# A banded attention and expert kernel on one core: TensorE's score steps in pairs

## The reference

```python
S = jnp.einsum('bcqd,bckd->bcqk', Qc, Kwin)              # local keys, 64 queries against 128
As = [S[:, :, qg, kg].reshape(bh, n, m)]                 # the band
for l in range(1, L + 1):                                # pooled keys, 8 a level
    Al = jnp.einsum('bcwd,bcpd->bcwp', q.reshape(bh, nbl, w, d), Kprev)
    As.append(Al.reshape(bh, n, p))
mn = maxes.min(axis=-1, keepdims=True)                   # the least of the five levels' maxima
exps = [jnp.exp(A - mn) for A in As]
...
out = jnp.einsum('bcqk,bckd->bcqd', Cfull, Vwin)         # value products, local
out = out + jnp.einsum('bcwp,bcpd->bcwd', Cs[l]..., Vprev)   # and pooled
...
x = x + _L0_attn_ref(_layernorm(x)); x = x + _L0_ffn_ref(_layernorm(x))
```

## Time and profile before

| | |
|---|---|
| median of 3 runs | 288.24 us (285.51 to 290.07) |
| the profiled execution's own time | 288.01 us |
| its span, first to last instruction | 286.2 us |
| outside the span | 1.8 us |
| TensorE busy | 273.4 us, 96% |
| mean granted TensorE clock | 0.964 of full speed |
| VectorE, ScalarE, GpSimd busy | 54%, 54%, 47% |
| attention units on TensorE | about 23 to 174 us |
| experts on TensorE | about 174 to 284 us |

### The profile page before, as it was taken

How to read it: one execution, slowest core, us unless ns; L and a number is a source line. 1 busy time by engine, 2 the same in 40 slices (tenths; PEclk the granted TensorE clock), 3 DMA queues, 4 the chain that set the end, 5 groups by cost and what they waited for, 6 DMA issues and landing times.

```text
span 286.2 us, 7298 instructions
## 1 busy us (share of the span) xinstructions
PE 273.4 (96%) x2705; PEld 226.5 (79%) x2705; DVE 154.6 (54%) x453; ACT 154.7 (54%) x316; POOL 135.8 (47%) x235
## 2 busy tenths in 40 slices
PE   7999999999999999993999999999999999999994
PEld 6868767887788988883888888788888678888883
DVE  7782644633344001322643162789886987777773
ACT  6765745534653432742487456544676555555551
POOL 7753302300041154140171301888885678888881
PEclk9999999989999975998999799999999999999999
DMA  7221176340097687558445011300000000000000
GB/s 212 61 58 60 57 171 192 81 126 2 11 289 277 168 229 170 145 155 165 128 144 154 26 22 21 85 10 10 10 11 9 10 11 10 9 11 18 11 9 19
DMA packets 19683, 24.14 MB, mean 84 GB/s; under 512 B 8312, under 2 KB 14456, under 8 KB 19648
## 3 DMA queue, kind: packets, MB, share of 16 engines
q1 hardware_dynamic: 18528, 22.80, 28.8%
q10 hardware_dynamic: 1120, 0.89, 1.2%
HBM read 11.91 MB, written 5.37 MB: 60 GB/s over the span
## 4 chain that ended last, share of the span: by engine, by line
PE 88%; DVE 3%; issue 3%; DMA 2%; SPq 1%; ACT 1%; POOL 1%; DVEq 0%; ACTq 0%; POOLq 0%
PE bank L1327 13%; PE bank L1140 12%; PE bank L1142 11%; PE bank L1141 11%; PE bank L1303 8%; PE bank L1306 6%; PE bank L1289 5%; PE bank L1221 3%; PE bank L1150 3%; PE bank L1331 2%; PE bank L1271 2%; PE bank L1237 2%; PE bank L1183 1%; DMA qst<-nshiftT 1%; PE bank L1171 1%
## 5 line engine op out<-in xcount | busy, mean ns | idle before, releaser
L752 POOL TENSOR_TENSOR work<-work 128x256 f32<-128x256 f32 x110 | 81.4, 744 | 31.2 <-DVE work L1123 18.3
L1123 DVE SCALAR_TENSOR_TENSOR work<-bank,comb,work 128x256 f32<-128x256 f32 x128 | 58.9, 480 | 24.7 <-ACT work L893 23.4
L893 ACT ACTIVATE work<-bank 128x256 f32<-128x256 f32 x128 | 48.4, 384 | 42.8 <-PE bank L1142 40.3
L868 ACT ACTIVATE work<-bank 128x512 f32<-128x512 f32 x64 | 37.7, 594 | 44.0 <-PE bank L1306 39.8
L1327 PE MATMUL bank<-work,vaug 128*64 128x64 f32 x1024 | 45.7, 235 | 0.0
L1327 PEld LDWEIGHTS bank<-work,vaug 128*64 128x64 f32 x1024 | 37.0, 144 | 9.0 <-issue 1.6
L658 POOL COPY vaug<-vwin 128x64 f32<-128x64 f32 x64 | 13.2, 250 | 51.7 <-PE bank L1331 51.5
L1303 PE MATMUL bank<-bar,ident_r 128*128 128x512 f32 x64 | 34.1, 533 | 0.0
L1306 PEld LDWEIGHTS bank<-qmk,kst 98*128 98x128 f32 x128 | 26.4, 206 | 4.3 <-issue 1.0
L1306 PE MATMUL bank<-qmk,kst 98*128 98x256 f32 x128 | 27.3, 297 | 0.0
L1141 PE MATMUL bank<-arena,xT_hi 128*128 128x512 f32 x64 | 25.1, 392 | 0.0
(11 more groups left out here) (217 smaller groups left out, 532.4 us busy)
## 6 DMA issues: line engine op xcount, KB each, us to landing
w_stage<-w SPq DMA_DIRECT2D x8, 512.0 KB, 3.9
qmk<-qst SPq DMA_DIRECT2D x20, 96.0 KB
qst<-arena SPq DMA_DIRECT2D x12, 128.0 KB, 3.8
kst<-arena SPq DMA_DIRECT2D x9, 128.0 KB, 3.2
qst<-q_rows SPq DMA_DIRECT2D x3, 384.0 KB, 4.2
qmk<-q_rows SPq DMA_DIRECT2D x12, 96.0 KB
p_rows<-kpool SPq DMA_DIRECT2D x2, 512.0 KB, 4.5
attT<-denom SPq DMA_DIRECT2D x8, 128.0 KB, 2.8
```

The lines of the kernel that those rows point to most:

```text
L752: gp.tensor_tensor(gacc[t % 2][:, :], gacc[t % 2][:, :], gtmp[(adds - 1) % TMP_RING][:, :], ALU.add).then_inc(acc_done, 1)
L868: act.activation(prob[lo % P_RING][:, :, :, :], bank[sc % SCORE_BANKS][:, :].rearrange("p (c j q) -> p c j q", c=2, j=GH), ACT.Exp).then_i ...
L893: act.activation(sig[hn % SIG_RING][:, :], bank[hn % HID_BANKS][:, HID:2 * HID], ACT.Sigmoid).then_inc(sig_done, 1)
L1123: dve.scalar_tensor_tensor(dst[:, :], bank[hn % HID_BANKS][:, 0:HID], comb[:, t, e:e + 1], sig[hn % SIG_RING][:, :], ALU.mult, ALU.mult).t ...
```

## The change

The loop over the ten score steps of a unit goes in pairs. Both score steps of a pair are put into the list first, then as many out steps as are due (two in the steady state), and then all side work that was hung beside the first and the second of them. The order among the score steps, among the out steps and among the side steps stays. SP's own order stays.

```diff
     for u in range(UNITS):
-        for i in range(SPU):
-            s.append(("score", u, i))
-            if unmasked:
-                mask()
-            if i >= 2:
-                local.append((u, i - 2))
-                unmasked.append((u, i - 2))
-            if len(local) > LAG:
+        for i in range(0, SPU, 2):
+            for n in (i, i + 1):
+                s.append(("score", u, n))
+                if unmasked:
+                    mask()
+                if i >= 2:
+                    local.append((u, n - 2))
+                    unmasked.append((u, n - 2))
+            while len(local) > LAG:
                 attend()
-            s += beside.get(u, {}).get(i, [])
-            if u + 1 < UNITS:
-                first = GUARD_AT[u]
-                if first <= i < first + 2:
-                    s.append(("guard", u + 1, i - first))
-                if i == first + 1:
-                    s.append(("shift", u + 1))
-                if i == first + 2:
-                    s.append(("shiftT", u + 1))
-                if i == first + 3:
-                    s.append(("shift load", u + 1))
+            for n in (i, i + 1):
+                s += beside.get(u, {}).get(n, [])
+                if u + 1 < UNITS:
+                    first = GUARD_AT[u]
+                    if first <= n < first + 2:
+                        s.append(("guard", u + 1, n - first))
+                    if n == first + 1:
+                        s.append(("shift", u + 1))
+                    if n == first + 2:
+                        s.append(("shiftT", u + 1))
+                    if n == first + 3:
+                        s.append(("shift load", u + 1))
```

## The result

| | before | changed |
|---|---|---|
| median beside each other | 287.78 us (285.51 to 290.07, 4 runs) | 294.50 us (292.98 to 297.00, 4 runs) |
| ratio, 95% interval | | 1.0269 (1.0160 to 1.0378) |
| profiled execution, its span | 288.01 us, 286.2 us | 294.15 us, 292.4 us |
| mean granted TensorE clock | 0.964 | 0.942 |

The account below looks back on a forecast made before the run. TensorE, busy 273.4 of 286.2 us, was taken as the bound. From 288.0 us, pairing wins 10.2, of which 7.8 are lost to later sources and growing waits, leaving −2.4: 285.6 us, range 281.5 to 290.0.

Parts of the forecast that it names:

- a rival with 0.22: New waits in units 1 and 2 bring more falls of TensorE's clock: 287.3 to 290 us, chance 0.22.
- other slices at half: Sign that the forecast is wrong: TensorE's clock at half in other slices than the four of the trace before.
- The price of a fall: One fall of TensorE's clock costs 1.8 us, from the 23rd slice of the trace before (1.4 to 2.1).
- The second row that lay ready: Stretch from 104 to 113 us before, at granted clock 0.50, where work takes up to twice as long.
- the section on short idle spells: Trainium skill: short idle spells between groups of products let the clock swing; by it the clock rival would be likeliest.
- the row of 22 to 43 us: Profile row before with the clock at 1.00, taken as evidence that half microsecond waits bring no falls.
- Ten microseconds of switches: Thirty fewer runs of out steps at 0.34 us each remove 10.2 us of TensorE's time.
- The lags: Delay against the old kernel, place by place: +1.2 at unit 1's pooled scores, +2.1 at unit 5's guard, −2.4 at the experts.
- The wait before `shiftT`: In unit 1, guard and `shiftT` of unit 2 now touch, so TensorE waits 1.15 us.
- The wait at the projection: TensorE's 4.6 us wait before the first projection grows to 6 or 7; most of the saving is lost here.
- The rival in which the switch is not what costs: Changing products saves nothing in the score and out steps and the delays stay: 291.5 us, chance 0.06.
- The first guard of unit 5: SP's queue carries the lag of unit 1's gather over whole: +2.1 us, TensorE's wait 1.5 to 2.

Follow-up runs that it names:

- e9: The kernel before with one stall of TensorE forced ahead of score step (4, 8): 302.01 and 291.32 us.
- e12: The kernel before once more, unchanged: 287.24 and 291.37 us.
- e5: The changed kernel run again unchanged, beside the kernel before: 293.86 us, ratio 1.0222.
- e13: The changed kernel run again unchanged in a later session, beside the kernel before: 294.0 us, ratio 1.0144.
- e4: The changed kernel with the old order in units 6 and 7, pairs in units 0 to 5: 301.24 us.
- e1: The changed kernel with the old order in units 0 and 1, pairs in units 2 to 7: 291.81 us.
- e6: The changed kernel with idle products in five of TensorE's waits: 287.52 us, ratio to the kernel before 1.0023.
- e7: The kernel before with idle products at the pooled scores, the guard of unit 5 and the projection: 292.67 us against 291.16.
- e11: Old order in units 0 and 1, pairs in units 2 to 7, idle products in three waits: 284.08 us against 288.33 before.

## Why the prediction was wrong

**The wrong step: a wait was priced at its length alone.** The sum kept the falls of the trace before, put the clock's part of the change at nothing, and left it to a rival with 0.22, whose worst value was 290. In the profiled execution it was +4.2 us of clock lost while busy. The sign that was named for this, other slices at half, was there. Over the traces of all kernels with the projection's wait unfilled (3.9 to 7.5 us, 12 traces) the clock fell there in all 12; with it filled, in none of 6. At the pooled scores of unit 1, 7 traces have the wait of about 2.7 us, and all fall within 3 us of its end; of 11 with less than 1 us or a filled wait, one does (e9, 0.82 us). At the guard of unit 4, 8 traces wait 1.65 to 1.86 us, and 7 fall. The forced stall of 1.57 us brought none, in 2. The filling experiments turn these counts into cause, though with wide margins: by the medians 3.6 us for the early waits, 5.1 for the late ones, 6.3 for all. The prediction named the first of these places and saw the other waits grow, and then gave no fall to any of them.

The same split as in the result, for every trace of the two kernels:

| us | busy, as if at full clock | clock lost while busy | TensorE waits |
|---|---|---|---|
| before: first trace, e12 | 263.4, 263.1 | 10.1, 7.8 | 12.8, 14.1 |
| changed: first trace, e5, e13 | 253.7, 254.1, 254.4 | 14.2, 15.2, 13.6 | 24.4, 24.4, 24.9 |

The price of a fall, 1.8 us from one slice of the earlier trace rows, fitted the short ones: three of the six falls of the first trace after took 3.4 us and lost 1.7. The falls behind the new waits were longer. In the three traces of the changed kernel the first fall lost 3.4, 3.4 and 5.1 us, and the one at the projection 5.1, 3.4 and 3.4, of which 2.6, 1.8 and 1.3 lay in the wait itself; e4's last fall lost 12. The second row that lay ready, 9 us at 0.50, would have given 4.5.

The Trainium skill, TensorE: Matmul & The Clock Gate, HAM oscillation — how this bites in real kernels, says that waits for transfers between groups of products throttle the engine again, so that the next group starts cold. The trace agrees, at a wait a little shorter than the 3 to 5 us of the page's example: the group behind the wait of 2.72 us ran at 0.50. The prediction weighed the section on short idle spells, and set it aside by the row of 22 to 43 us. That row could not bear this: its one wait above half a microsecond is the 0.86 before the pooled scores, and these begin at 43.11, behind the row's end. What waits of about a microsecond do, the runs leave open. In unit 7 a fall begins within 3 us of the first `gatelog` in 16 of the 18 traces: in all 13 where it waits (0.79 to 0.99 us in 12, 2.19 in e4), but also in 3 of the 5 where it doesn't, the first trace of before among them; no run filled this wait. The 1.18 to 1.29 us before `shiftT` brought a fall in none of 8 traces.

**A low draw.** The sum started from 288.0, the first executions of the kernel before had 287.8 as a mean and all 61 have 292.1. So some 4 of the 8.9 us between forecast and measurement are luck. From 292.1 the same sum would have given 289.7, against the changed kernel's mean of 294.1: the miss of the mechanism is 4 to 5 us. In the split by mean clock over the 57 and 16 executions whose clock is known the lost clock is 1.6 us more after, uncertain by 2.1, and the rest 0.2 more, where the prediction had 2.4 less. So it is shown that filling the waits of the changed kernel takes 4 to 6 us off its time; that it loses more clock than the kernel before on average is not.

**Ten microseconds of switches.** Right: 0.24, 0.47 and 0.43 us in the chain. Busy time as if at full clock is 9.6 us less, against 10.2, and 8.7 to 9.6 less between any two traces of the table.

**The lags.** TensorE's waits grew by 11.6 us, not 7.8. The first guard of unit 4 waits 1.80 us where the prediction has no wait: it followed SP's queue from the gather of unit 1 to the guard of unit 5 and passed over the queries for unit 4 that SP moves in between. e1 has this wait too (1.82), so it comes from the pairs behind unit 1. The pooled scores of unit 1 came at +2.1, not +1.2 (`kp` was later: TensorE waited 0.60 us at 31.93 for an exponential on ScalarE, and 0.27 at 35.03). ScalarE held TensorE for 1.03 us at 152.00 and 0.65 at 158.33, `gatelog` for 0.95 at 163.62: 2.6 us, where 1.2 were taken for all three. Of the first, ScalarE's queue shows why (start, us, idle before):

```profile
149.82 1.65 ACT L854 ACTIVATE xnorm<-xres,nmr,rstd 128x127 f32<-128x127 f32 x4 [2.11 <-POOL nmr L643]
151.38 1.05 ACT L870 ACTIVATE work<-bank 128x512 f32<-128x512 f32 x2
```

Both exponentials of the pair now queue behind `apply2`, and that waits 2.11 us for GpSimd.

**What was right.** The wait before `shiftT`: 1.19 us (predicted 1.15). The wait at the projection, nearly: 7.22 (6 to 7). It grew by 2.6 us, more than any other. That most of the saving would be lost there is too much: 2.6 is less than a quarter of what the waits grew by. The rival in which the switch is not what costs is out by the chain. e1 confirms the delays of units 0 and 1: without them the rest is 1.3 us under the kernel before, and the guard of unit 2 is back at 49.06.

**The first guard of unit 5** was to come at +2.1 with a wait of 1.5 to 2 us. Its transfers were issued from 104.11 to 107.38, but TensorE, as late itself and at half clock before it, reached it only at 112.90, +9.6, and did not wait. At full clock (e6) it waited 0.71 us at 106.86, +3.6.

**Left open.** Why the kernel before varied from 282.4 to 303.9 us and the changed one only from 289.9 to 300.4. Its lost clock explains the size of it (its rest hardly moves), but not why some executions escape the falls: 23 of 61 executions before were under 290 us, 1 of 16 after. The regular waits of the pairs would explain that the low ones are gone; it isn't shown. Nor is it known what ends a fall, after 3.4 us here and 24 there, nor what brings those that begin at 61 to 69 us, in 12 traces, with no wait of half a microsecond in the 3 us before any of them, nor those behind a `gatelog` that didn't wait.

## What to carry to other kernels

Removing work from the bounding engine turns it into waiting wherever the engine stands behind a chain that doesn't get shorter, and in this kernel a wait of TensorE of two or three microseconds cost more than its length: ask of each wait that grows what runs right behind it, and what it costs at half clock. Reorder only where the freed time can be used (here units 2 to 7), and try to fill the waits that remain with idle products; the two together gave the fastest version, though in the old order filling showed no gain. And take more than four executions of a kernel whose clock falls, of the kernel before above all: four of them lay 4 us under the mean of 61. Split each time into lost clock and rest, for the rest of one kernel spreads by about a microsecond around its mean where the time spreads over twenty; and in a trace, count the lost clock only where the engine is busy.

## What was unexpected of the hardware

Time followed the clock almost alone: 61 executions of one program spread over 21.5 us, with a rest of 277.1 to 277.4 in each session's mean. The clock stayed at half while TensorE was busy without a gap for 24 us (e4), 20 (e9), 17 (e7 and e11) and 10 (before), and elsewhere for 3.4. The counts of waits and falls hold for this kernel only, and length alone doesn't order them: 0.79 to 0.99 us at `gatelog` with a fall in 12 of 12 traces (and without a wait in 3 of 5), 1.18 to 1.29 before `shiftT` in 0 of 8, the forced 1.57 in 0 of 2, 1.65 to 1.86 at the guard of unit 4 in 7 of 8, 2.7 at the pooled scores in 7 of 7.
